# An interaction tower in fp32: self doubles multiplied whole, dense inputs written into zT by DMA, z groups that end with bursts, look-ups tile by tile in block 0

## The reference

```python
e = jnp.stack([tbl_0[ids[:, 0]], ..., tbl_31[ids[:, 31]]], axis=1)   # 1024 x 32 x 64
p = e[:, ROW]                                  # ROW, COL: the 496 pairs of fields
q = e[:, COL]
kp = jnp.einsum('bpj,ipj->bpi', p, kernel)     # a 64x64 matrix for each pair
z = jnp.sum(kp * q, axis=-1)                   # 1024 x 496
h = jnp.concatenate([z, dense_ctx], axis=1)    # 1024 x 512
h = jnp.maximum(h @ W_top1 + b_top1, 0.0)      # 512
h = jnp.maximum(h @ W_top2 + b_top2, 0.0)      # 256
y = h @ W_top3
```

## Time and profile before

| | us |
|---|---|
| median of three runs | 469.12 |
| the runs | 468.0, 469.12 and one of 1582.94 |
| the profiled execution, its own time | 469.35 |
| its span, first to last instruction | 467.4 |
| outside the span | 1.95 |
| TensorE matmuls busy | 446.4 |
| VectorE busy | 302.5 |
| POOL busy | 242.4, its last look-up begins at 321.66 |
| ScalarE busy | 34.1 |

### The profile page before, as it was taken

One profiled execution on the slowest core, in us unless ns is written; L12 is line 12 of the kernel. 1 busy time (PEld: TensorE's weight loads), 2 busy tenths in 40 slices (PEclk: granted clock), 3 DMA queues, 4 the chain that ended last, 5 costly groups with the idle time before them and its releaser, 6 DMA issues.

```text
span 467.4 us, 8271 instructions
## 1 busy us (share of the span) xinstructions
PE 446.4 (95%) x3544; PEld 274.7 (59%) x3544; DVE 302.5 (65%) x287; ACT 34.1 (7%) x55; POOL 242.4 (52%) x262
## 2 busy tenths in 40 slices
PE   7976999999999999999999999999999999999996
PEld 7965555666655466666565666666555656643442
DVE  1033687777787787677878777777878868870000
ACT  1001000001001000110000100000100000002112
POOL 6777777777777777777777777774000000000000
PEclk9989899999999999999999999999999999999999
DMA  2244447111111111111111111110000000000000
GB/s 84 83 128 137 153 175 250 44 29 27 25 29 27 28 29 25 30 27 27 29 27 25 30 27 28 29 27 20 1 1 2 0 1 1 1 1 0 0 0 0
DMA packets 11146, 18.82 MB, mean 40 GB/s; under 512 B 4820, under 2 KB 5080, under 8 KB 10856
## 3 DMA queue, kind: packets, MB, share of 16 engines
q0 software_dynamic: 8192, 8.40, 7.9%
q1 hardware_dynamic: 2920, 9.91, 6.0%
HBM read 18.29 MB, written 0.00 MB: 39 GB/s over the span
## 4 chain that ended last, share of the span: by engine, by line
PE 86%; POOL 6%; issue 3%; DVE 2%; DMA 1%; ACT 1%; DVEq 0%
PE u_ps L318 45%; PE z_ps L344 24%; POOL nat L187 6%; PE u_ps L361 6%; PE t_ps L301 4%; PE u_ps L325 3%; PE u_ps L382 3%; DVE prod L279 1%; PE z_ps L339 1%; ACT zT L221 1%; DMA nat<-tbl,ids_sb 1%; DMA ids_sb<-ids 0%; DVE prod L273 0%; PE u_ps L388 0%; ACT k_sb L244 0%
## 5 line engine op out<-in xcount | busy, mean ns | idle before, releaser
L273 DVE TENSOR_TENSOR prod<-u_ps,rows 128x1024 f32<-128x1024 f32 x240 | 277.6, 1216 | 109.5 <-PE u_ps L318 109.3
L187 POOL DMA_INDIRECT nat<-tbl,ids_sb x256 | 241.7, 944 | 79.4 <-issue 76.8
L318 PE MATMUL u_ps<-rows,k_sb 64*128 64x256 f32 x1920 | 228.6, 386 | 5.6 <-issue 2.2
L318 PEld LDWEIGHTS u_ps<-rows,k_sb 64*128 64x128 f32 x1920 | 181.8, 188 | 59.8 <-DVE prod L273 24.4
L344 PE MATMUL z_ps<-prod,sel 128*32 128x512 f32 x992 | 120.9, 602 | 1.4 <-ACT zT L221 1.4
L344 PEld LDWEIGHTS z_ps<-prod,sel 128*32 128x32 f32 x992 | 26.0, 110 | 60.1 <-issue 38.3
L216 ACT ACTIVATE rows<-t_ps 128x512 f32<-128x512 f32 x32 | 19.1, 597 | 277.8 <-PE t_ps L301 277.8
L284 DVE COPY y_sb<-u_ps 1x256 f32<-1x256 f32 x2 | 0.8, 424 | 45.6 <-PE u_ps L388 45.6
L301 PEld LDWEIGHTS t_ps<-ident,nat 128*128 128x128 f32 x128 | 13.4, 141 | 27.4 <-issue 22.5
L361 PE MATMUL u_ps<-zT,w_sb 128*128 128x512 f32 x64 | 28.0, 595 | 1.1 <-DVE prod L279 1.1
L293 PE MATMUL u_ps<-ident 128*128 128x128 f32 x200 | 25.8, 294 | 3.3 <-DVE sel_dense L261 3.3
(11 more groups left out here) (18 smaller groups left out, 10.8 us busy)
## 6 DMA issues: line engine op xcount, KB each, us to landing
nat<-tbl,ids_sb POOLq DMA_INDIRECT x256
k_sb<-kern SPq DMA_DIRECT2D x3, 768.0 KB, 4.5
k_sb<-kern SPq DMA_DIRECT2D x2, 640.0 KB, 4.5
k_sb<-kern SPq DMA_DIRECT2D x1, 1152.0 KB, 5.4
k_sb<-kern SPq DMA_DIRECT2D x2, 512.0 KB, 4.4
w_sb<-w SPq DMA_DIRECT2D x1, 1024.0 KB, 7.9
k_sb<-kern SPq DMA_DIRECT2D x1, 896.0 KB
k_sb<-kern SPq DMA_DIRECT2D x3, 256.0 KB, 3.2
```

Source lines behind the costliest of these rows:

```text
L187: pool.indirect_dma_start(nat[:, i % LANES, t, n, h * EMBED:(h + 1) * EMBED], None, tables[f], bass.IndirectOffsetOnAxis(ids_sb[:, col:col ...
L273: op = nc.vector.tensor_tensor(to, u, by.unsqueeze(1).to_broadcast([P, 2, 2, SIZE]), ALU.mult)
L318: op = nc.tensor.matmul(u[:, h, :], k_sb[part, d, side, :], rows[part, tile, cols], start=True, stop=True)
```

## The change

- **Self doubles.** ScalarE copies the eight operands of a self double side by side into a new tile by_self (gather_by_self, two activations of 64x1024, three doubles ahead), and VectorE multiplies the double in one instruction of 128x1024. It waits for by_self_ready; ScalarE waits for the product of the self double before.
- **Dense inputs.** The L339 matmuls, dense_sb and sel_dense are gone. After a block's second group is in zT, SP issues four small DMAs that write the block's dense inputs into the free rows of zT; the first layer waits for them.
- **Bursts.** quads_behind goes by the block: bursts begin anew in each block, a block's last double is followed by two quads (three in block 3), and the block's thirty-first quad follows the fourth double of the next block. Every z group ends with a burst, and all sums stand ahead of the first layer.
- **Tiles.** The unit is a tile, not a step: POOL's ring is eight tiles with a semaphore each. Block 0's sixteen tiles are transposed and copied one by one, those of later blocks in pairs.
- **The planner** has other rules and constants. It reckons when a tile has landed (5.0 us for a tile, 2.4 us to land), and places a pair ahead of a run of four doubles when the pair has landed 1 us before the planner's own time (2 us before).

```diff
-URING, PRING, NAT, LANES, AT_ONCE = 3, 8, 16, 4, 2
+URING, PRING, RING = 3, 8, 8
 BURST = 4
 def quads_behind(n):
-    return range(max(0, (n + 1) // 2 - BURST), (n + 1) // 2 - BURST // 2) if n % BURST == BURST - 1 else ()
-STEPS = BLOCKS * TILES // AT_ONCE
-def step_of(b, tile):
-    return (b * TILES + tile) // AT_ONCE
-def lane_count(i):
-    return 32 * AT_ONCE * SUBS * (i // LANES + 1)
-assert NAT == AT_ONCE * SUBS * LANES
+    b, d = divmod(n, ND)
+    first = b * QUADS
+    if d == ND - 1:
+        return range(first + QUADS - 3, first + QUADS - (b < BLOCKS - 1))
+    if d == BURST - 1:
+        return range(max(0, first - 1), first)
+    return range(first + d // 2 - 3, first + d // 2 - 1) if d % BURST == BURST - 1 else ()
...
-K_AFTER_STEP = [max(0, (tile - 3) // AT_ONCE) for tile in range(2, TILES)]
-LOOK_UP, LANDING = 1.25, 5.0
+K_AFTER_TILE = [max(0, tile - 3) for tile in range(2, TILES)]
+START, TILE_TIME, LANDING = 3.0, 5.0, 2.4
...
 def plan():
-    there = [LANDING + LOOK_UP * 2 * AT_ONCE * SUBS * (i + 1) for i in range(STEPS)]
-    now, step, before, fill = 2.5, 0, [], [0] * STEPS
+    issued, there, done = START, [], []
+    now, before, fill = 2.5, [], [0] * LOOKED_UP
+    def landed(m):
+        nonlocal issued
+        while len(there) <= m:
+            n = len(there)
+            issued = max(issued, done[n - RING] if n >= RING else 0) + TILE_TIME
+            there.append(issued + LANDING)
+        return there[m]
     for b in range(BLOCKS):
         for d in range(ND):
-            here, needed = [], step_of(b, tile_of(d))
-            while step < STEPS and (step <= needed or not here and (b * ND + d) % BURST == 0 and there[step] + 2 <= now):
-                if there[step] > now:
-                    fill[step] = int(0.8 * (there[step] - now) / FILL)
-                    now = there[step]
-                now += TURN + TRANSPOSE * AT_ONCE * SUBS + (0.8 if step == needed else 0)
-                here.append(step)
-                step += 1
+            here, needed = [], b * TILES + tile_of(d)
+            while len(done) < LOOKED_UP:
+                m = len(done)
+                count = 2 if m >= TILES and m % 2 == 0 else 1
+                if m > needed and (here or d % BURST or landed(m + count - 1) + 1 > now):
+                    break
+                last = landed(m + count - 1)
+                if last > now:
+                    fill[m] = int(0.8 * (last - now) / FILL)
+                    now = last
+                now += TURN + TRANSPOSE * SUBS * count + (0.8 if m + count > needed else 0)
+                here.append((m, count))
+                done.extend([now] * count)
             before.append(here)
             now += DOUBLE + 2 * TURN / BURST
     return before, fill
-STEPS_BEFORE, FILL_BEFORE = plan()
+TILES_BEFORE, FILL_BEFORE = plan()
...
+            for m in range(LOOKED_UP):
+                b, tile = divmod(m, TILES)
+                if m >= RING:
+                    pool.wait_ge(transposed, m - RING + 1)
+                for n in range(SUBS):
+                    for h in range(2):
+                        f = 2 * tile + h
...
+            for b in range(BLOCKS):
+                sp.wait_ge(z_out, (b + 1) * ZGROUPS)
+                cols = slice(b * SIZE, (b + 1) * SIZE)
+                for k in range(4):
+                    row = 32 * k + 2 * DENSE_SLOT
+                    sp.dma_start(zT[row:row + 2, ZROWS - 2:ZROWS, cols], dense[k, :, :, cols]).then_inc(dense_in[b], 16)
...
+            def gather_by_self(b, tile):
+                n = b * ND + DOUBLES.index((tile, None))
+                act.wait_ge(rows_ready, b * TILES + tile + 1)
+                if n > DOUBLES.index((TILES // 2 - 1, None)):
+                    act.wait_ge(prod_ready, max(m for m in range(n) if DOUBLES[m % ND][1] is None) + 1)
+                flat = by_self.rearrange("p s b n -> p (s b) n")
+                for half in range(2):
+                    part, t = slice(EMBED * half, EMBED * (half + 1)), self_tile(tile, 0, half, 0)
+                    nc.scalar.activation(flat[part], rows[part, t:t + 7:2, b * SIZE:(b + 1) * SIZE], ACT.Copy).then_inc(by_self_ready, 1)
...
             for n in range(BLOCKS * ND):
-                for i in STEPS_BEFORE[n]:
-                    rows_out(i)
+                for m, count in TILES_BEFORE[n]:
+                    rows_out(m, count)
+                b, d = divmod(n + 3, ND)
+                if b < BLOCKS and DOUBLES[d][1] is None:
+                    gather_by_self(b, DOUBLES[d][0])
...
-                    for bank in range(2):
-                        for half in range(2):
-                            part = slice(EMBED * half, EMBED * (half + 1))
-                            t = self_tile(one, bank, half, 0)
-                            op = nc.vector.tensor_tensor(to[part, bank], u[part, bank], rows[part, t:t + 5:4, cols], ALU.mult)
+                    dve.wait_ge(by_self_ready, 2 * sum(DOUBLES[m % ND][1] is None for m in range(n + 1)))
+                    op = nc.vector.tensor_tensor(to, u, by_self.rearrange("p s b n -> p b s n"), ALU.mult)
...
+            def transpose(m, count):
+                for t in range(m, m + count):
+                    pe.wait_ge(gathered[t % RING], lane_count(t))
+                if m > 0:
+                    pe.wait_ge(rows_ready, m)
+                for t in range(count):
                     for s in range(SUBS):
-                        op = nc.tensor.transpose(t_ps[:, t, s, :], nat[:, i % LANES, t, s, :], ident[:])
-                op.then_inc(transposed, 1)
+                        op = nc.tensor.transpose(t_ps[:, t, s, :], nat[:, (m + t) % RING, s, :], ident[:])
+                op.then_inc(transposed, count)
...
-                if q == SLOTS:
-                    if b == 0:
-                        pe.wait_ge(dense_in, 16)
-                    for side in range(2):
-                        for k in range(4):
-                            nc.tensor.matmul(z_ps[32 * k:32 * k + 32, side, :], sel_dense[:, side, k, :],
-                                             dense_sb[:, b * SIZE:(b + 1) * SIZE], start=side == 0, stop=False)
...
-            pe.wait_ge(z_out, (BLOCKS - 1) * ZGROUPS)
+            pe.wait_ge(z_out, (BLOCKS - 2) * ZGROUPS)
+            for b in range(BLOCKS - 2):
+                pe.wait_ge(dense_in[b], 64)
...
-            for n in range(3):
+            for n in range(4):
                 h1_product(n)
-            for quad in range(BLOCKS * QUADS - BURST // 2, BLOCKS * QUADS):
-                add_up(quad)
-            h1_product(3)
             pe.wait_ge(z_out, BLOCKS * ZGROUPS)
+            for b in range(BLOCKS - 2, BLOCKS):
+                pe.wait_ge(dense_in[b], 64)
```

More of the change, by code:

```diff
@@ L150, in tower @@
         u_ps = pb("u_ps", [P, URING, 2, 2, SIZE])
-        t_ps = pb("t_ps", [P, AT_ONCE, SUBS, P])
+        t_ps = pb("t_ps", [P, 2, SUBS, P])
         z_ps = pb("z_ps", [P, 2, SIZE])
@@ L177, in _ @@
             pool.wait_ge(ids_in, 16)
[L178 to L191, removed]
+            for m in range(LOOKED_UP):
[5 more added lines that the diff above has]
+                        f = 2 * tile + h
+                        col = (b * SUBS + n) * FIELDS + f
+                        pool.indirect_dma_start(
+                            nat[:, m % RING, n, h * EMBED:(h + 1) * EMBED], None, tables[f],
+                            bass.IndirectOffsetOnAxis(ids_sb[:, col:col + 1], 0)).then_inc(gathered[m % RING], 16)
+            for m in range(LOOKED_UP - RING, LOOKED_UP):
+                pool.wait_ge(gathered[m % RING], lane_count(m))
         @block.sync
@@ L212, in _, with rows_out @@
         def _(act):
-            def rows_out(i):
-                b, pair = divmod(i, TILES // AT_ONCE)
-                act.wait_ge(transposed, i + 1)
-                nc.scalar.activation(rows[:, pair * AT_ONCE:(pair + 1) * AT_ONCE, b * SIZE:(b + 1) * SIZE],
-                                     t_ps.rearrange("p t n c -> p t (n c)"), ACT.Copy).then_inc(rows_ready, 1)
+            def rows_out(m, count):
+                b, tile = divmod(m, TILES)
+                act.wait_ge(transposed, m + count)
+                nc.scalar.activation(rows[:, tile:tile + count, b * SIZE:(b + 1) * SIZE],
+                                     t_ps[:, 0:count].rearrange("p t n c -> p t (n c)"), ACT.Copy).then_inc(rows_ready, count)
+            def gather_by_self(b, tile):
[7 more added lines that the diff above has]
+                    nc.scalar.activation(flat[part], rows[part, t:t + 7:2, b * SIZE:(b + 1) * SIZE], ACT.Copy).then_inc(by_self_ready, 1)
             def z_evacuate(b, g):
@@ L234, in h1_out @@
                 nc.scalar.activation(h1T(m, cols), h_ps(n), ACT.Relu, bias=b1_sb[:, m:m + 1]).then_inc(h1_ready, 1)
-            for n in range(3):
-                h1_out(n)
-            z_evacuate(BLOCKS - 1, ZGROUPS - 1)
-            for n in range(3, 8):
+            for n in range(8):
                 h1_out(n)
```

(2 more changed lines are left out.)

48 lines of the change are left out of this document (18 added, 30 removed).

## The result

The changed kernel takes 471.92 us in the median of five runs (471.87 to 473.49), against 469.12 before: a ratio of 1.0077, with a 95% interval of 1.0045 to 1.0109. The forecast was 473.8 within 471.2 to 476.0. It is slower by 0.8%, clear of the noise, and within the 2% that were called "about the same".

The account below looks back on a forecast made before the run. It took POOL's look-ups to set the pace up to n = 180: 9.6 us later, less 6.7 gained, plus 0.2, is 3.1; with 1.6 for half clock 474.05 profiled, so 473.8 us, range 471.2 to 476.0.

Parts of the forecast that it names:

- The table decides: TensorE's transposes, placed earlier by the planner, wait for POOL's look-ups until tile 63 lands; n = 180 begins at 324.68.
- 9.6 was the term: Start of n = 180, ahead of the last run placed behind transposes: 9.6 us later than before.
- look-ups don't bind: Rival for the stretch to n = 180: TensorE doesn't wait for POOL, all gains count, 15 us, 454; 4%.
- The gains behind n = 180: From n = 180 to the first layer: 6.7 us saved, less 0.2 for one more cut run.
- The term for the stall of the self double: Block 3's self double that is first of a run: whole product removes 0.97 us idle, taken as 1.0.
- the end (1.2 was the term): Last burst to first layer: the last product is done while two of three quads run, saving 1.2 us.
- in each place (0.9 and 0.9): Group ends: 0.9 us saved for a burst cut by ScalarE's z_ps copy, 0.9 for a group's dense matmuls.
- What should cost nothing: ScalarE's by_self copies and the dense DMAs: taken as 0, with 2 us as the copies' other end.
- The clock: TensorE's half clock behind the last look-up wait, ahead of n = 180: 1.6 us lost, 0 as low end.
- this way out: If the wait ahead of n = 168 lowers the clock, that ahead of 180 shrinks to 0.6 and costs nothing.
- the rival with 34%: The clock stays up at the last wait, ahead of n = 180: 472.2 us; 34%.
- The start: Block 0: single tiles bring n = 7 forward 5 us, with tile 6 at 39.3; all swallowed by n = 52.

Follow-up runs that it names:

- e4: Changed kernel with the planner's 0.8 us only where the tile is needed at once, VectorE's four products back and no ScalarE copies: 455.04 us, ratio 0.9708.
- e5: Changed kernel with the planner's 0.8 us line mended, bursts counted over all doubles as before, last four quads behind the last double: 455.94 us, ratio 0.9732.
- e6: Changed kernel with the planner's 0.8 us line mended and the dense inputs by matmuls into z_ps as before: 456.94 us, ratio 0.9771.
- e3_fill: Changed kernel with 4 or 8 fill matmuls ahead of each waiting pair from n = 70: 625.04 us, ratio 0.9658 to the kernel before.
- s1_late: Changed kernel with the planner's 0.8 us line mended and nothing else: 614.83 us against 646.11 for the kernel before, ratio 0.9529.
- r2_before_early: Kernel before with only the changed kernel's early places of the transposes from tile 18 on: 646.1 us, ratio 1.0017.

## Why the prediction was right, and where it was off

**The table decides: right.** The forecast rested on one comparison, POOL's 219.8 us for 44 tiles against at most 206.2 us of TensorE's work in the same stretch. The nine waits stand where it had listed them, 14.0 us in sum behind block 0 (it had said 15 to 26 with those of block 0, which are 4.0 more), though three of them are 0.80 to 0.94 us, under the 1 it had given. The last transposes begin at 324.17, and it had given 324.1. The run of n = 180 begins at 324.73, 9.66 us later than in the earlier trace rows, where 9.6 was the term. And e4, e5 and e6 show the cause by experiment: what they share is one line of the planner; the waits are gone, and the time is 15 to 17 us lower although a different part of the change is missing from each. The run with this one edit and nothing else is missing in the usual condition. The "look-ups don't bind" rival, priced at 454, is what that mended kernel would come to by the estimate of 453.8.

**The gains behind n = 180: right, a little small.** From the start of n = 180 to the first layer it took 98.93 us after, and 415.92 + 3.06 - 315.07 + 1.85 = 105.76 before, with the sums that stood in the first layer. That is 6.8 saved, where 6.7 - 0.2 = 6.5 was the sum. The term for the stall of the self double took only its 0.97 us of idle. It was also put down to the whole product alone, and the new bursts remove it by themselves: in e4, with four products, nothing waits behind that self double, since it is no longer the first of its run; in e5, where it is the first, the whole product does it. The two parts share this 1.0 us. Of the single terms, e4 gives 1.25 for the end (1.2 was the term) and e5 and e6 show 0.93 and 0.86 in each place (0.9 and 0.9). All eight layer products in one row also took 27.57 us (423.66 to 451.23), 0.2 less than in two pieces.

**What should cost nothing: right.** VectorE waited for no by_self copy, the layer for no dense DMA.

**The clock: the term that was off.** "I take it as 1.6" was the term that was mis-sized: in the profiled execution half clock did come, but behind other waits, and behind the last one it cost nothing. The windows of the changed kernel behind four waits of over 2.2 us:

```profile
144.30:148.60 4.30, 4.26 (x40) 3.48 (x44) 2.52 (x3) 2.71 (x3) 3.37 (x4) 1.00 0.14 30
184.30:188.50 4.20, 4.12 (x22) 3.31 (x24) 1.03 (x1) 0.60 (x1) 3.29 (x4) 0.59 0.15 28
...
284.00:288.00 4.00, 3.91 (x36) 3.43 (x36) 2.17 (x2) 0.60 (x1) 2.99 (x4) 1.00 0.13 29
...
304.00:308.50 4.50, 4.39 (x26) 3.58 (x28) 1.25 (x2) 0.60 (x1) 3.51 (x4) 0.63 0.16 32
```

Waits of 2.23 and 2.29 us left the clock at its full level, 2.4 GHz (a granted clock of 1.00), waits of 2.41 and 2.28 were followed by half clock, 1.2 GHz, for a part of the window (0.59 and 0.63 on average). The price was as read: 184.38 to 190.22 is 5.84 us and 304.11 to 309.84 is 5.73, where 284.09 to 288.30 took 4.21, so 1.6 and 1.5. After 304 the loss made TensorE later, which shortened the wait ahead of n = 180 to 0.80, and behind that one the four doubles took 3.65 from start to start, the price at full clock. The forecast had named this way out and then set it aside by the argument that the wait ahead of 168 would shrink likewise; that holds only if every wait of this length lowers the clock, and half of them did. Without the 1.6, its sum is 472.2, the rival with 34%, against 471.92. The three runs at 471.9 and the two at 473.2 and 473.5 would fit a last wait with and without half clock, but only one execution has a trace, and e3_fill, which was to tell this apart, met the other condition. The time lies near the low end of the range, which held because it had kept 0 as this term's low end.

The Trainium skill, in "TensorE: Matmul & The Clock Gate", section "HAM oscillation — how this bites in real kernels", describes a loop in which each tile behind a DMA wait starts at the lower clock; the waits of that loop are longer than these. The forecast took this for every new wait, and it held behind two of the nine: behind the five of 0.80 to 1.10 us the transposes took 0.63, as at full clock. Whether transposes count differently, which the forecast took from the same page, no run here shows.

**The start** differed in detail. The forecast had tile 6 at 39.3; its transposes began at 40.04, behind a wait for the look-ups, 3.14 us after the last of them was issued at 36.90, and not the 2.39 of the earlier trace rows. Nothing of this reaches the end.

## What to carry to other kernels

Two suppliers with nearly the same pace need both clocks read: POOL's busy share was 52% and looked harmless, while in the stretch from tile 18 to tile 63 its look-ups took 219.8 us where TensorE took 228.2, 4% short of binding. In a program with a fixed order, a wait that isn't needed yet holds up everything behind it, so work that depends on a transfer belongs as late as its user allows, not as early as a planner believes the transfer done; and a planner's clock must be checked against the trace (here it added 0.8 us to every group, where the transposes of a pair took 0.59 in all, and with that line mended the loss of 0.8% became a gain of 2.3% to 2.9% even with a part of the change missing). Gains of TensorE ahead of such a wait are worth nothing, and only those behind the last one count.

## What the runs showed that was not expected

- Idle times of nearly the same length, 2.23, 2.28, 2.29 and 2.41 us in one execution, led to half clock in two cases and not in the two others; the length alone doesn't tell it.
- There was a condition, met on three chips and absent ten minutes earlier on one of them, in which the kernel before took 638 to 653 us instead of 468 to 470. In s1_late TensorE was busy 164 of 200 us while look-ups ran and 60 of 60 behind them; r2_before_early has a gap of 5.45 us within a run of doubles. The profile names no releaser for such gaps, and their cause is open.
- In that condition the single tiles in block 0 were worth 24 us.
